# Early-fusion transformer kernel on one core: three residual additions on GpSimd tied to row-maximum matmuls, a fourth to a normalisation, and a new stage order

## What is computed

```
h = tok(x, channel_weights)                 # patch sums
h = concatenate([h, txt], axis=1)           # 273 tokens x 192
h = h + L0_attn(layernorm(h), ...)          # 12 heads, quantised scores, no softmax
h = h + L0_ffn(layernorm(h), ...)           # routed attention for 41 tokens, mix, then MLP
h = h + L1_attn(layernorm(h), ...)          # 12 heads, softmax
h = h + L1_ffn(layernorm(h), ...)           # shared expert + 3 routed experts
```

## Time and profile before

| | us |
|---|---|
| median of 3 runs | 4869.73 (4862.02 to 4880.92) |
| profiled execution, its own time | 4867.58 |
| its span, first to last instruction | 4865.9 |
| PE busy | 4159.1 (85%) |
| DVE busy | 2695.0 (55%) |
| ACT busy | 1762.4 (36%) |
| POOL busy | 416.9 (9%) |
| mean granted clock of PE | 0.853 of full speed |

### The profile page before, as it was taken

How to read it: one execution, slowest core, us unless ns; L and a number is a source line. 1 busy time by engine, 2 the same in 40 slices (tenths; PEclk the granted TensorE clock), 3 DMA queues, 4 the chain that set the end, 5 groups by cost and what they waited for, 6 DMA issues and landing times.

```text
span 4865.9 us, 70034 instructions
## 1 busy us (share of the span) xinstructions
PE 4159.1 (85%) x27744; PEld 3253.4 (67%) x27744; DVE 2695.0 (55%) x7217; ACT 1762.4 (36%) x2774; POOL 416.9 (9%) x523
## 2 busy tenths in 40 slices
PE   2778888889888888888888888898888888888888
PEld 1556667677666776666677666677667677666666
DVE  2446555555655555655555656555656555655443
ACT  1224333334333344333334333334333333433332
POOL 2100011000001000001000001010001010001000
PEclk8668888888888888879888889888888988888888
DMA  4111111101111101101101111101111101111000
GB/s 112 32 25 34 32 26 36 31 22 33 32 26 36 36 17 34 35 22 36 34 19 34 35 22 36 36 18 33 36 29 29 36 21 29 36 25 16 13 13 4
DMA packets 154045, 147.12 MB, mean 30 GB/s; under 512 B 64359, under 2 KB 132026, under 8 KB 153722
## 3 DMA queue, kind: packets, MB, share of 16 engines
q1 hardware_dynamic: 153722, 142.64, 13.7%
HBM read 87.28 MB, written 7.91 MB: 20 GB/s over the span
## 4 chain that ended last, share of the span: by engine, by line
PE 63%; DVE 18%; SPq 5%; ACT 4%; DMA 4%; issue 3%; POOL 3%; POOLq 0%; DVEq 0%; ACTq 0%
PE area_a L1023 12%; PE area_n L1031 11%; PE area_b L1023 8%; PE area_m L1031 7%; SPq L451 4%; PE area_n L1248 4%; DMA k1s<-scratch 3%; PE area_n L1055 3%; DVE mx L927 3%; PE area_m L1198 3%; ACT pT_both L655 2%; PE area_b L1046 2%; PE area_a L1106 2%; DVE xn L730 2%; DVE scratch L938 1%
## 5 line engine op out<-in xcount | busy, mean ns | idle before, releaser
L927 DVE TENSOR_REDUCE mx<-area_n 91x1 f32<-91x273 f32 x1152 | 465.2, 432 | 273.7 <-PE area_n L1248 259.1
L1248 PE MATMUL area_n<-k1s,q1s 96*91 96x273 bf16 x1152 | 352.8, 364 | 226.1 <-DVE mx L927 124.2
L1031 PE MATMUL area_n<-w_dn,hid 128*91 128x192 f32 x2304 | 493.9, 379 | 41.3 <-DVE mrow L932 33.5
L1031 PEld LDWEIGHTS area_n<-w_dn,hid 128*91 128x91 f32 x2304 | 425.9, 190 | 89.4 <-issue 55.1
L1023 PE MATMUL area_a<-xT,w_gu 96*128 96x273 f32 x1536 | 409.0, 409 | 66.5 <-DVE y L887 38.2
L1023 PE MATMUL area_b<-xT,w_gu 96*128 96x273 f32 x1536 | 435.8, 431 | 0.0
L1248 PEld LDWEIGHTS area_n<-k1s,q1s 96*91 96x91 bf16 x1152 | 147.6, 146 | 399.0 <-DVE mx L927 229.3
L1023 PEld LDWEIGHTS area_a<-xT,w_gu 96*128 96x128 f32 x1536 | 283.9, 193 | 149.4 <-DVE y L887 48.0
L1023 PEld LDWEIGHTS area_b<-xT,w_gu 96*128 96x128 f32 x1536 | 308.2, 206 | 70.7 <-issue 0.5
L600 ACT ACTIVATE pa<-area_a,scal 91x820 bf16<-91x820 f32 x192 | 180.3, 939 | 313.5 <-PE area_a L1106 278.8
L990 DVE SCALAR_TENSOR_TENSOR outb<-area_n,cwt,outb 91x192 f32<-91x192 f32 x288 | 102.0, 407 | 272.9 <-PE area_n L1031 272.9
(11 more groups left out here) (242 smaller groups left out, 7776.7 us busy)
## 6 DMA issues: line engine op xcount, KB each, us to landing
img<-in_x SPq DMA_DIRECT2D x192, 392.0 KB, 3.5
q1s<-scratch SPq DMA_DIRECT2D x192, 102.4 KB, 3.4
k1s<-scratch SPq DMA_DIRECT2D x192, 102.4 KB, 4.5
out<-outb SPq DMA_DIRECT2D x32, 204.8 KB
q0s<-scratch SPq DMA_DIRECT2D x128, 25.6 KB, 3.8
k0s<-scratch SPq DMA_DIRECT2D x128, 25.6 KB, 2.2
pooled<-pooled_dram SPq DMA_DIRECT2D x128, 9.2 KB
tokens<-in_txt SPq DMA_DIRECT2D x32, 57.8 KB
```

Of the source, the lines that this page charges most:

```text
L927: v.tensor_reduce(mx[:, k:k + 1], N[0:TC, k % 2, 0:T], AX.X, ALU.max)\
L1031: last = mm(by_token(x)[:, c, :], lhs(i, c), w_, start=(i == 0), stop=(i == len(w) - 1))
L1248: mm(N[0:TC, k % 2, 0:T], q1s[0:SROWS, hh, c * TC:(c + 1) * TC], k1s[0:SROWS, hh, :], start=True, stop=True).then_inc(full["N"], 1)
```

## The change

Two new stages, `r2` and `r3`, take over the additions that stood in `n0n` and `n1s`; `r1` stays. All three first wait, by `await_last`, until PE has filled area N for the last `mx` stage named ahead of them in the turn. In a turn without `mx` stages that wait is absent. The addition in `n3s` now waits for `xn_ready["B"]`, which DVE raises at the end of `n3n`. The list `TURN` is written anew.

```diff
-tok n4s n4n n4f cw n0s n1s n2n n0n qk1.0 qk1.1 v2 n0f qk0.0 qk0.1 pool.0 n2f ey.0 v1 ez.0 ey.1 mx.0 mx.1 mx.2 n1n mx.3
+tok n4s n4n n4f cw n0s n1s n2n n0n qk1.0 qk1.1 v2 n0f qk0.0 pool.0 qk0.1 n2f ey.0 v1 ez.0 ey.1 mx.0 mx.1 mx.2 n1n gate
...
+            def await_last(self, x, stage, name):
+
+                before = [s_ for s_ in self.stages[:self.stages.index(stage)] if s_.startswith(name)]
+                if before:
+                    self.await_full(x, before[-1])
...
-                    elif stage == "n0n":
-
+                    elif stage == "n1s":
+                        inv_std("B", stage, 2, 0, twice=True)
+                    elif stage == "r2":
+
+                        t.await_last("N", stage, "mx")
                         pool.wait_ge(xn_ready["A"], t.done(stage))
                         add_row(tokens0, tokens0, bproj0).then_inc(base0_ready, 1)
-                    elif stage == "n1s":
-                        inv_std("B", stage, 2, 0, twice=True)
+                    elif stage == "r3":
+                        t.await_last("N", stage, "mx")
                         add_row(hb0, h0, bf2).then_inc(hb0_ready, 1)
                     elif stage == "n3s":
                         inv_std("B", stage, 2, 1)
                         pool.wait_ge(hb0_ready, t.done(stage))
+                        pool.wait_ge(xn_ready["B"], t.image(stage) * 2 + 2)
                         g.tensor_tensor(hb0[:, :, :], hb0[:, :, :], hs[:, :, :], ALU.add).then_inc(res0_ready, 1)
...
                     elif stage == "r1":
+                        t.await_last("N", stage, "mx")
                         if "dy.0" in t.stages:
                             t.await_taken("N", "dy.0")
                         add_row(hb1, h1, bproj1).then_inc(hb1_ready, 1)
```

More of the change, by code:

```diff
@@ L51 @@
 TURN = """
-tok n4s n4n n4f cw n0s n1s n2n n0n qk1.0 qk1.1 v2 n0f qk0.0 qk0.1 pool.0 n2f ey.0 v1 ez.0 ey.1 mx.0 mx.1 mx.2 n1n mx.3
[L53 to L59, removed]
+tok n4s n4n n4f cw n0s n1s n2n n0n qk1.0 qk1.1 v2 n0f qk0.0 pool.0 qk0.1 n2f ey.0 v1 ez.0 ey.1 mx.0 mx.1 mx.2 n1n gate
+mx.3 ez.1 mx.4 pool.1 k1 mx.5 v0 a0.0 mx.6 mx.7 ey.2 cl.0 cl.1 ez.2 mx.8 r3 mx.9 mx.10 rta a0.1 cl.2 dy.0 cl.3 pk0
+a0.2 mx.11 mx.12 mx.13 mx.14 mx.15 pk1 ey.3 ez.3 mx.16 r2 mx.17 gt mx.18 vs mx.19 pv.0 mx.20 og.0 mx.21 s1.0 mx.22
+mx.23 s1.1 r1 mx.24 ey.4 ez.4 ey.5 mx.25 ez.5 t1.0 mx.26 mx.27 t1.1 mx.28 rtb mx.29 cl.4 mx.30 cl.5 a0.3 c1 mx.31
+mx.32 mx.33 mx.34 mx.35 ct pool.2 mt dy.1 a2.0 pool.3 wo a2.1 a2.2 a2.3 a2.4 cl.6 a2.5 cl.7 pw.0 os.0 a2.6 pool.4 pv.1
+og.1 a2.7 ob.0 a2.8 a2.9 pw.1 os.1 a2.10 a2.11 ob.1 mg n3s n3n ey.6 ey.7 pool.5 ez.6 pw.2 os.2 ey.8 ez.7 ez.8 n3f a0.4
+cl.8 cl.9 dy.2 f0.0 f0.1 ob.2 f0.2 ey.9 ez.9 pr1 n5s a0.5 n5n cl.10 cl.11 fd ey.10 pv.2 ey.11 og.2 ez.10 n5f ez.11 pr0
+dy.3 rtr
 """.split()
 OFFSET = {"pool": -1}
-OFFSET.update({x: 0 for x in "tok n0s n0n n0f qk0 v0 vs a0 cl pv og pr0".split()})
-OFFSET.update({x: 1 for x in ("n1s n1n n2n n2f gate k1 v1 rta rtb pk0 gt pk1 s1 t1 c1 ct wo mg n3s n3n n3f f0 fd".split())})
+OFFSET.update({x: 0 for x in "r2 tok n0s n0n n0f qk0 v0 vs a0 cl pv og pr0".split()})
+OFFSET.update({x: 1 for x in ("r3 n1s n1n n2n n2f gate k1 v1 rta rtb pk0 gt pk1 s1 t1 c1 ct wo mg n3s n3n n3f f0 fd".split())})
 OFFSET.update({x: 2 for x in "n4s n4n n4f r1 qk1 v2 mx mt a2 pw os ob pr1 n5s n5n n5f rtr".split()})
```

## The result

The changed kernel takes 4828.52 us, median of 18 runs (4793.07 to 4858.72); the kernel before, beside it on the same chip, 4868.95 us, median of 18 (4857.69 to 4884.17). The ratio is 0.9916, with a 95% interval from 0.9899 to 0.9932: 0.8% faster, about 40 us. The forecast was 4812 us, so direction and size were right. The runs of the changed kernel spread over 1.4%, those of before over 0.5%, and the profiled execution is the fastest of the 18. Its trace is good for what happens in a turn; the total is read from the median.

A forecast was written before the change was run, and what follows sets the result against it. PE, busy 85% of the span, was taken to set the length, other engines mattering only through its waits. 4867.6 - 66.5 + 11.2 = 4812.3, forecast 4812 us; 8-in-10 range 4745 to 4870.

The forecast's parts named there:

- two early stalls: DVE's `n2n` and first split's cast, each held 1.09 us by a POOL addition ahead of the stack DMAs: 66.5 us removed.
- third stall: DVE's `n3n`, held about 1.09 us by a POOL addition; removing it gains 0, bounds 16 us either way.
- order, without `pool.2`: Other stage moves (`pool.0`, `c1`, `gt`, `pv.0`, `og.0`, `pool.3`, `pool.4`, `gate`): taken as 0, `c1` group's bounds 14 us either way.
- `pool.2` ahead of `mt`: Image slice delays `mt` and PE's `dy.1` by 0.35 us a turn: 11.2 us added, bounds 0 and 34.
- `r1` behind `mx.23`: Addition at its new place beside `s1`: taken as 0, at most 35 us if the small scaling is held.
- all of it comes off PE's wait: The 2.18 us a turn of early stalls wholly shortens PE's wait for the stack, since the shortest found is 2.29.
- The prediction's own sign of being wrong: Stalls vanish but the stack's wait does not shrink by 2 us, or it shrinks and the turns do not.
- The first rival: Behind `mx.0`, a shorter wait keeps the clock high; `k1` saves 1.8 us a turn, 56 us more (4756 us); chance 0.17.
- 66.5 us removed: Gain from ending the two early stalls ahead of the stack DMAs: 61 x 1.09 us.
- The rivals on the clock: Behind `mx.0`: clock stays high (4756 us, chance 0.17), or turns meet more low stretches, 3.1 us each (4908 us, 0.12).
- I take 0: Additions at their new places hold nothing on DVE, mostly PSUM maxima there: cost 0, upper bound 35 us.
- this rival: Small scaling in `s1` is held 1.09 us by `r1`'s addition, delaying ACT's exponential and `ey.4`: +35 us (4847 us); chance 0.13.

The follow-up runs named there:

- the other pair: Two kernels with `r1` behind `mx.25`, differing only in `pool.2` ahead of or behind `mt`: 0.9771 and 0.9689 of the kernel before.
- e3_early_two: Kernel before with only the additions `r3` and `r2` moved, behind `mx.8` and `mx.16`; `r1`, `n3s` and the order as before: 4758.69 us, ratio 0.9783.
- e1_adds_only: Kernel before with all four additions as in the change, the stage order otherwise as before: 4810.87 us, ratio 0.9886.
- e5_r1_back: Changed kernel with only `r1` back behind `pk0` and without its wait: 4728.50 us, ratio 0.9720 to the kernel before.
- e11_third_too: `e3_early_two` with the addition of `n3s` also waiting for `n3n`: 4760.55 us, ratio 0.9789 to the kernel before.
- e6_pool2_back: `e5_r1_back` with the image slice `pool.2` behind `mt` again: 4709.04 us, ratio 0.9696 to the kernel before.
- e7_fill_mx: `e5_r1_back` with eight unused 128x64 products put into PE's wait for the stack ahead of `mx.0`: 4785.40 us, ratio 0.9854 to the kernel before.

## Why the prediction was right, point by point

Put in a chain, each step by the two kernels that differ in it, in parts of 4865 us:

| step | predicted, us | measured, us | from ratios |
|---|---|---|---|
| two early stalls gone | -66.5 | -105.6 | 1 to 0.9783 |
| third stall gone | 0 | +3 (not told from 0) | 0.9783 to 0.9789 |
| order, without `pool.2` | 0, bounds 14 | -45 | 0.9789 to 0.9696 |
| `pool.2` ahead of `mt` | +11.2 | +12 (+40 in the other pair) | 0.9696 to 0.9720 |
| `r1` behind `mx.23` | 0, at most 35 | +95 | 0.9720 to 0.9916 |
| sum | -55.3 | -41 | 0.9916 |

By the intervals of the ratios a step is known to within 8 to 18 us.

**Right.** The mechanism, that DVE is held to the end of POOL's addition and that both stalls stand ahead of the stack's DMAs: `n2n` at 0.95, the cast at 0.44, the first DMA 2.16 us earlier in the turn. The third stall is free within the bounds of 16 us that the prediction gave.

**Right in sign, not shown in size: `pool.2`.** The wait ahead of `dy.1` that was to grow by 0.35 us a turn grew from 33.5 to 38.8 us in all, 5 us instead of 11. The times give 12 us in one pair, not told from nothing, and 40 in the other. That the first lies on the forecast's 11.2 is no confirmation.

**Wrong: "all of it comes off PE's wait".** The prediction's own sign of being wrong was a wait for the stack that does not shrink by 2 us, and that came: it shrank by 0.98 us in the turn shown and by 45.0 us in all, 1.5 a turn, and 1.90 us lie outside the 0.1 to 1.2 that were forecast. The step took PE's arrival at the wait as fixed. PE came there 1.16 us earlier, and the two parts together make the 2.1 us by which `mx.0` starts earlier in the turn (at 19.14 instead of 21.29).

**The first rival** ("`k1` at about 2 us") did not come at its place: one such `k1` of the changed kernel takes 3.64 us (it was 3.85), and the row of its matmuls sums to 109.9 us against 121.3, 11 us in place of the 56 that the rival asked for.

**Wrong in size: "66.5 us removed".** The idle time is about right: from before to `e3_early_two` PE's idle time falls by 58.8 us (706.8 to 648.0, span less busy). The term left out PE's own work, which got 37.4 us shorter with the same matmuls (mean granted clock 0.859 against 0.853). The rivals on the clock had it at one place behind `mx.0`; what moved was the length of whole turns, in steps of about 3.3 us. That halves don't add fits these steps (one stall of 1.09 us a turn gave 34 us, two gave 106), though no run shows why a turn takes one length or the other.

**Wrong: "I take 0" for the additions' new places.** The bound of 35 us, "held like the others", was the duration of the hold (33.2 us in the trace, well sized) but not its price, 70 to 95 us in the new order. In the old order, where 22 us are held in `e1_adds_only` (32.9 - 10.9), the price is 47. The prediction set against this rival that "`ey.4` has a few tenths of slack". It has them without the hold. The same stretch in a turn of `e5_r1_back`, DVE, ACT and PE:

```profile
1395.54 0.71 DVE L878 TENSOR_REDUCE smx<-area_a 123x2 f32<-123x546 f32 x1
...
1396.49 0.87 ACT L633 ACTIVATE scratch<-area_a,smx 123x273 f32<-123x273 f32 x2 [2.66 <-DVE smx L879]
...
1397.98 3.48 PE L1033 MATMUL area_a<-xT,w_gu 96*128 96x273 f32 x8
1401.30 2.01 PE L1033 MATMUL area_b<-xT,w_gu 96*128 96x273 f32 x8
```

`ey.4` writes area A once ACT's exponential has read it. Here that ends at 1396.49 + 0.87 = 1397.36, and `ey.4` starts 0.62 us later. In the changed kernel it ends at 1276.21 + 0.87 = 1277.08, and `ey.4` starts at 1277.13, right behind: a hold of 1.18 us is more than the slack. Counted from the maximum of `s1.0`, `ey.4` starts after 3.05 us instead of 2.44. PE hardly idles for that; its waits ahead of `ey.4` for the exponential are, in the whole changed kernel,

```profile
PE area_a L1034 <- ACT scratch L634: 1.9, 8, 0.2
```

Most of the price is in the clock. Windows with PE's busy time and clock, first of the changed kernel, then of `e5_r1_back`:

```profile
1271.00:1274.00 3.00, 2.76 (x25) 0.75 0.00 0
1274.00:1277.00 3.00, 2.75 (x7) 0.50 0.02 5
1277.00:1280.00 3.00, 2.90 (x7) 0.50 0.00 0
1280.00:1283.00 3.00, 3.00 (x9) 0.54 0.00 0
...
1392.30:1395.30 3.00, 2.76 (x31) 0.81 0.00 0
1395.30:1398.30 3.00, 2.67 (x8) 0.50 0.02 5
1398.30:1401.30 3.00, 3.00 (x9) 0.56 0.00 0
```

In both turns the clock falls ahead of the maximum of `s1.0`, in the changed kernel before `r1`'s addition starts at 1274.76. So the hold doesn't make it fall. It comes back later: by the shares of these windows 8.7 us after that maximum instead of 5.4. `ey.4` and `ez.4` take 4.01 and 2.91 us where they take 3.48 and 2.01 in `e5_r1_back`, and 2.11 and 2.01 in the turn of the kernel before that starts at 1962.83. What the changed kernel's turn had gained on that one, 3.60 us at `s1.0`, was down to 0.23 us at its end. Not every turn is like this: `ey.4` takes 4.0 us in 22 of the 30 turns of the changed kernel in which both stand together, and 2.1 in the other 8, and at most 3.5 in `e5_r1_back`. That the hold keeps the clock low for longer is read from these rows; why it does so stays open.

The rival had been given 0.13, with "no row shows so small an operation beside an addition" against it. The rule that the rows did show, one-input scalings and casts in SBUF held to the addition's end, named no size.

**Wrong: the order at 0.** With the stalls in place the new order is 0.37% slower, with them gone it is 0.69% faster (`e11_third_too` to `e5_r1_back`, both without a hold). The sum of opposite signs that the prediction set to zero is in the waits: PE waits less for row maxima and more for `hid`. First `e11_third_too`, then `e6_pool2_back`:

```profile
PE area_n L1258 <- DVE mx L937: 129.9, 235, 2.2
```

```profile
PE area_n L1258 <- DVE mx L937: 95.9, 201, 1.7
...
PE area_b L1177 <- DVE hid L990: 21.7, 30, 0.8
```

That is 34 us less and 21.7 more (in `e11_third_too` area B never waits for `hid`). PE's idle time as a whole differs by 6.8 us and its busy time by 21.9 in these two executions, of which that of `e11_third_too` is 22 us faster than its median; the mechanism that lets an order be worth more once the stalls are gone was not isolated.

The forecast is close by luck, because two errors of opposite sign met: 84 us too little gain (39 at the stalls, 45 in the order) and 95 us too little loss for the hold. The median missed it by 16 us.

**What the change left on the table.** With `r1` where it was and `pool.2` behind `mt` (`e6_pool2_back`) the kernel takes 4709 us, 3.0% less than before and 2.2% less than the changed kernel. The kernels with other places of `r1` and a filled gap (0.9689, 0.9674) are not told apart from it.

## What to carry to other kernels

When an addition moves on GpSimd, list every VectorE operation of the kinds seen held (here scalings and casts from SBUF to SBUF) that can fall into its 1.4 us at the new place, the smallest too: an operation of 0.17 us was held for as long as a large one (1.18 and 1.09 us), and what matters is who waits for it. A term that is free "in itself" still deserves one kernel of its own, since two of these terms were wrong by more than the net result. And in a kernel whose clock changes level, price a microsecond in front of the bounding engine by measuring it: here it was worth one (one stall: 34 us for 33) to three (the hold: 95 us for 33).

## What was not expected of the hardware

- A 123x2 scaling beside an addition took 1.35 us instead of 0.17, held to the addition's end. The maxima out of PSUM beside the same kind of addition kept their 0.43 us (three in 1.28 us from 1270.01, the addition running from 1269.39 for 1.41).
- The lengths of most turns lie near steps: 136.9, 140.2, 143.4, 146.7 us for the same instructions. With the filler matmuls of `e7_fill_mx` 25 of the 29 full turns were 143.3 to 143.4 us long, where those of the fastest kernels change from one turn to the next: in `e6_pool2_back` one of 136.86 us with 122.70 of PE's work at a clock of 0.90, another of 143.77 with 127.40 at 0.87.

- Filling PE's idle time at two places with matmuls of 64 columns did not keep its clock up, and at one of them the kernel was 1.3% slower.
